# A selective scan and a routed feed-forward block on one core: a shorter routing of tokens, and one product of every second chunk moved from GpSimd to VectorE

## The chip, the core and the metric

The kernel runs on one core of a Trainium2 chip. A core has a matrix engine (TensorE, PE in the profile), a vector engine (VectorE, DVE), a scalar engine (ScalarE, ACT), a general engine (GpSimd, POOL) and a queue that issues transfers (SyncE, SP). The engines run side by side, each through its own instructions in order, and wait for one another by semaphores. The metric is the device time of one execution in microseconds, lower is better. All data are float32; some matmul operands are rounded to fp32r, a form that the matrix engine takes in fewer passes.

## The reference, cut to what matters

The input is 4 sequences of 2048 tokens of width 256. A first block normalises each token, runs a state space scan over time (512 channels, 16 states each) and adds its result to the input. A second block does this, with a router and four small low-rank experts:

```python
logits = einsum('bsd,ed->bse', x, Wg) + bg
scores = softmax(logits)
topv, topi = top_k(scores, 2)
w = sum(one_hot(topi, 4) * topv[..., None], axis=-2)
base = einsum('bsd,fd->bsf', x, Wi)
lora_low = einsum('bsd,erd->bser', x, A)          # 4 experts x rank 4
lora = einsum('bser,efr->bsef', lora_low, B)
h = relu(base[:, :, None, :] + lora)
expert_out = einsum('bsef,df->bsed', h, Wo)
out = einsum('bse,bsed->bsd', w, expert_out)
```

For each token the two experts with the largest logits count. The kernel ranks the four logits, keeps the low-rank row of the best and of the second, and computes only these two. The scan itself is, for each channel and state, `h = h * exp(dt * A) + (dt * x) * B`, and `y = sum over states of h * C`.

## The kernel before

The tokens are cut into 16 chunks of 512 (`NC`), the four sequences in turn. A chunk goes through 16 steps (`STEPS`); a step covers 128 channels (four groups of 32, `J`) and 4 of the 16 states, so that 128 partitions hold 32 channels by 4 states, and four tiles of 128 x 512 lie side by side. In each step:

- GpSimd computes the input of the scan for all four tiles (`times_b`, line 1470, 128 x 2048: `dx_rep` by `b_rep`).
- ScalarE computes the four decays `exp(dt * A)` into the PSUM tiles `decay` (line 1203).
- VectorE scans the four tiles, one instruction each (line 1395). The line reads `decay` from PSUM and `hs` from SBUF.
- The states are multiplied by C. The lower two tiles are always VectorE's (line 1382, 128 x 1024). The upper two are GpSimd's where the step's number modulo 4 is below 3 (`POOL_STEPS`, line 1482), and VectorE's in steps 3, 7, 11 and 15.
- ScalarE copies the last column of each half into `state` (`keep_state`, line 1217). Only then may it write the next step's decays over that half. It waits for the product by C of that half where the scan left the states in `decay`, and for the scan alone where GpSimd takes the product.
- TensorE sums the states (line 998).

On every engine, what else a chunk needs (projections, layer norms, gate, router, feed-forward) is cut into jobs of one letter and one number, and hand-made tables say after which tile of which step each job stands: `PE_SIDE`, `ACT_SIDE`, `DVE_SIDE` and so on for the chunks in general, `..._LAST` for the last chunk, `..._END` for the tail after it. The four cells of a row are the places behind tiles 0 to 3 of that step. `pre`, `post` and `late` mean that the job works for the next chunk, the one before, or the one before that. No planner moves anything: an engine that waits in one job delays all that stands behind it.

The jobs that the change touches:

- H (VectorE, `route`, lines 1325 to 1361; it stands in steps 10 to 12): ten parts. It adds the bias to the logits twice, once into SBUF and once into PSUM, compares all pairs (greater, equal, the lower triangle `tri` for ties), sums to ranks, makes masks, multiplies them into the low-rank rows, and writes the result four times for each choice into `pk`: two copies rounded to fp32r (line 1359), two with what the rounding left (line 1361). Every VectorE instruction of it with two tensors as inputs has one of them in PSUM.
- I (TensorE 951, ScalarE 1170, step 13): four transposes of `pk` and one copy into `low_t`.
- J and S: the experts' matmuls, which read `low_t`.
- X (ScalarE 1166) and M, W: the exponentials and weights of the two choices.
- C0, C1 (step 8, not changed, but of a like form): ScalarE rounds the projection into `dt_st` (line 1093); TensorE subtracts that from the same PSUM bank (line 878); ScalarE copies what is left (line 1086).

Of the kernel before, what the change touches and what calls it, by code (L numbers as in the profile page):

```python
# [41 lines left out]
BOUND = 41.0  # L42

# [156 lines left out]
    "S1 main |  |  | ",  # L200
    " |  |  | H0 post, Y1 main",
    "S2 main, H1 post | H2 post, K2 late, H3 post | H4 post | H5 post",
    "H6 post | H7 post, H8 post | H9 post | M0 post",
# [1355 lines left out]
```

## Time and profile before

| what | us |
|---|---|
| median of 3 runs | 1856.04 |
| the runs | 1853.64, 1856.04, 1858.43 |
| the profiled execution: its own time | 1855.82 |
| its span, first to last instruction | 1854.0 |
| TensorE busy | 1624.7 (88%) |
| VectorE busy | 1763.7 (95%) |
| ScalarE busy | 1503.9 (81%) |
| GpSimd busy | 1714.5 (92%) |

A chunk takes about 108.4 us. Busy time counts an instruction from its start to its end, and neighbours overlap by up to a tenth of a microsecond or more, so what an instruction costs its engine is read from its start to the start of the one behind it. The shares are averages that hold the start (in which GpSimd waits 40.0 us for its first tile) and the tail (from about 1776 us, in which TensorE works and the others wait).

### The profile page before, as it was taken

The numbers are of one execution on the slowest core, as the hardware profiler recorded it, in microseconds if no ns is written. First come the engines' busy times: TensorE is split into PE (matmuls) and PEld (weight loads), VectorE is DVE, ScalarE is ACT, GpSimd is POOL, SyncE is SP. The second block draws the span as 40 slices with busy tenths as digits, with TensorE's granted clock in tenths as the row PEclk, the third lists the DMA queues.
The fourth block names the chain that finished last, engine by engine and source line by source line (L and its number), as shares of the span: only waits on it lengthen the run. The fifth ranks groups of instructions, "written<-read, shape, count | busy, mean of one in ns | idle before, by whom it ended". The sixth has DMA issues, their size and how long they took to land.

```text
span 1854.0 us, 26281 instructions
## 1 busy us (share of the span) xinstructions
PE 1624.7 (88%) x7052; PEld 830.2 (45%) x7052; DVE 1763.7 (95%) x2060; ACT 1503.9 (81%) x3113; POOL 1714.5 (92%) x649
## 2 busy tenths in 40 slices
PE   6657689998998999889898989989899998988999
PEld 3213244444444444444444444444444444444465
DVE  5999999999999999999999999999999999999951
ACT  4776889888898988889898888979888897988643
POOL 1999999999999999999999999999999999999910
PEclk9767799999999999999999999999999999999999
DMA  6655565655656565554747556574665657475200
GB/s 211 138 137 139 118 154 140 157 129 138 152 107 174 131 166 128 141 141 108 181 116 170 140 129 146 111 185 118 165 143 127 137 118 190 99 167 136 63 7 18
DMA packets 150070, 249.07 MB, mean 134 GB/s; under 512 B 22432, under 2 KB 47264, under 8 KB 149408
## 3 DMA queue, kind: packets, MB, share of 16 engines
q1 hardware_dynamic: 145456, 231.09, 51.0%
q0 software_dynamic: 4464, 16.25, 4.6%
q8 instruction: 61, 1.00, 0.2%
q14 instruction: 89, 0.73, 0.1%
HBM read 188.01 MB, written 42.99 MB: 125 GB/s over the span
## 4 chain that ended last, share of the span: by engine, by line
DVE 35%; PE 18%; issue 17%; POOL 16%; ACT 7%; DMA 2%; SPq 1%; DVEq 0%; POOLq 0%; ACTq 0%
DVE decay L1395 15%; POOL hs L1470 10%; DVE hs L1382 9%; DVE hs L1395 7%; POOL hs L1482 4%; PE bank L914 3%; PE bank L962 3%; ACT decay L1203 3%; PE y_ps L998 2%; PE bank L984 2%; POOL z_dt L1450 2%; PE bank L918 1%; DMA b_rep<-bc_scratch 1%; DVE silu L1282 1%; PE bank L979 1%
## 5 line engine op out<-in xcount | busy, mean ns | idle before, releaser
L1470 POOL TENSOR_TENSOR hs<-dx_rep,b_rep 128x2048 f32<-128x2048 f32 x255 | 1188.9, 4678 | 43.1 <-DVE hs L1411 40.0
L1395 DVE TENSOR_TENSOR_SCAN decay<-decay,state,hs 128x512 f32<-128x512 f32 x640 | 791.5, 1270 | 4.9 <-ACT decay L1203 3.9
L1203 ACT ACTIVATE decay<-dt_rep,a_sb 128x512 f32<-128x512 f32 x1024 | 692.5, 685 | 20.6 <-DVE dx_rep L1409 1.8
L1395 DVE TENSOR_TENSOR_SCAN hs<-decay,state,hs 128x512 f32<-128x512 f32 x384 | 485.8, 1265 | 1.3 <-ACT decay L1203 0.8
L1482 POOL TENSOR_TENSOR hs<-hs,c_rep 128x1024 f32<-128x1024 f32 x192 | 476.5, 2482 | 6.0 <-ACT state L1217 5.8
L1382 DVE TENSOR_TENSOR hs<-decay,c_rep 128x1024 f32<-128x1024 f32 x320 | 383.7, 1199 | 0.0
L998 PE MATMUL y_ps<-hs,nsum 128*32 128x512 f32 x2048 | 292.2, 645 | 53.5 <-POOL hs L1482 44.8
L914 PE MATMUL bank<-xn_t,w_in_sb 128*128 128x512 f32 x512 | 252.6, 622 | 10.3 <-DVE silu L1282 3.5
L962 PE MATMUL bank<-w_i_sb,x_t 128*128 128x512 f32 x492 | 249.6, 631 | 8.2 <-DVE silu L1282 6.9
L984 PE MATMUL bank<-w_o_sb,r_t 128*128 128x256 f32 x944 | 217.0, 383 | 4.7 <-ACT r_t L1186 2.7
L984 PEld LDWEIGHTS bank<-w_o_sb,r_t 128*128 128x128 f32 x944 | 178.8, 191 | 56.2 <-issue 28.5
L1217 ACT COPY state<-decay 128x2 f32<-128x2 f32 x320 | 50.6, 158 | 171.0 <-DVE hs L1382 166.3
L914 PEld LDWEIGHTS bank<-xn_t,w_in_sb 128*128 128x128 f32 x512 | 91.9, 195 | 132.4 <-issue 90.4
L962 PEld LDWEIGHTS bank<-w_i_sb,x_t 128*128 128x128 f32 x492 | 89.9, 199 | 121.6 <-issue 89.4
L979 PE MATMUL bank<-ident,r 128*128 128x128 f32 x920 | 120.8, 278 | 6.4 <-ACT r L1181 4.3
L979 PEld LDWEIGHTS bank<-ident,r 128*128 128x128 f32 x920 | 100.6, 141 | 52.2 <-DVE x L1298 15.6
L936 PE MATMUL bank<-w_out_sb,gated 128*128 128x256 f32 x496 | 118.0, 380 | 0.3 <-DVE gated L1287 0.3
L998 PEld LDWEIGHTS y_ps<-hs,nsum 128*32 128x32 f32 x2048 | 41.9, 110 | 148.2 <-issue 125.6
L1181 ACT ACTIVATE r<-bank,wgt 128x512 f32<-128x512 f32 x123 | 83.1, 675 | 23.5 <-PE bank L885 23.4
L936 PEld LDWEIGHTS bank<-w_out_sb,gated 128*128 128x128 f32 x496 | 94.5, 191 | 14.0 <-DVE gated L1287 0.7
L1177 ACT ACTIVATE r<-bank,wgt 128x512 f32<-128x512 f32 x123 | 83.1, 676 | 20.0 <-PE bank L966 19.6
L1186 ACT COPY r_t<-bank 128x512 f32<-128x512 f32 x119 | 69.4, 583 | 17.8 <-PE bank L979 13.4
(170 smaller groups left out, 1823.9 us busy)
## 6 DMA issues: line engine op xcount, KB each, us to landing
dx_rep<-rep_scratch SPq DMA_DIRECT2D x252, 256.0 KB, 4.7
dt_rep<-rep_scratch SPq DMA_DIRECT2D x252, 256.0 KB, 7.6
b_rep<-bc_scratch SPq DMA_DIRECT2D x256, 64.0 KB, 4.0
c_rep<-bc_scratch SPq DMA_DIRECT2D x256, 64.0 KB, 2.4
rep_scratch<-z_dt SPq DMA_DIRECT2D x64, 256.0 KB, 2.6
rep_scratch<-e_dt SPq DMA_DIRECT2D x64, 256.0 KB, 2.7
e_dt<-z_dt POOLq DMA_DIRECT2D x31, 512.0 KB, 4.6
xin<-in_u SPq DMA_DIRECT2D x16, 512.0 KB, 4.1
```

What stands on the lines that cost most here:

```text
L914: mm = pe.matmul(ps[:], w_in_sb[:, k, col:col + P], xn_t[odd][:, k, :], start=k == 0, stop=k == KD - 1)
L936: pe.matmul(ps[:, cols], gated[odd][:, k, i * P:(i + 1) * P], w_out_sb[:, k, :], start=k == 0 and is_last(q) and i % 2 == 0, stop=False, s ...
L962: pe.matmul(ps[:], x2_t[odd][:, k, t * P:(t + 1) * P], w_i_sb[:, k, cols], start=k == 0, stop=False, skip_group_check=is_last(q))
L979: mm = pe.matmul(ps[:, f * P:(f + 1) * P], r[i % 2][:, f * P:(f + 1) * P], ident[:], start=r is r1, stop=r is r2, is_transpose=True)
L984: mm = pe.matmul(ps[:, 0:D], r_t[:, f, :], w_o_sb[:, f, :], start=f == 0, stop=f == NF - 1)
L998: mm = pe.matmul(y_ps[32 * j:32 * j + 32, :], nsum[:], hs[s % 4][:, j, :], start=k == 0, stop=k == KG - 1, skip_group_check=True)
L1177: nc.scalar.activation(r1[i % 2][:], ps[:], ACT.Relu, scale=wgt[odd][:, 0, i // 2:i // 2 + 1]).then_inc(r1_ready, 1)
L1203: nc.scalar.activation(decay[:, j, :], dt_rep[m % 2][:, j, :], ACT.Exp, scale=a_sb[:, J * s + j:J * s + j + 1]).then_inc(decay_ready, 1)
L1382: v.tensor_tensor(hs[s % 4][:, js, :], decay[:, js, :], c_rep[:, k, :].unsqueeze(1).to_broadcast([P, 2, T]), ALU.mult).then_inc(prod_vecto ...
L1395: v.tensor_tensor_scan(hs[s % 4][:, j, :] if kept else decay[:, j, :], decay[:, j, :], hs[s % 4][:, j, :], state[:, b, n:n + 1], ALU.mult, ...
L1470: nc.gpsimd.tensor_tensor(hs[s % 4][:], dx_rep[m % 2][:], b_rep[:, k, :].unsqueeze(1).to_broadcast([P, J, T]), ALU.mult).then_inc(input_re ...
L1482: nc.gpsimd.tensor_tensor(hs[s % 4][:, 2:4, :], hs[s % 4][:, 2:4, :], c_rep[:, k, :].unsqueeze(1).to_broadcast([P, 2, T]), ALU.mult).then_ ...
```

## The change

1. The routing has seven parts (H0 to H6). The biased logits are written once, in SBUF. A difference of all pairs replaces the two comparisons; ties are settled by comparing with a tiny number instead of zero. Both masks come from one instruction. One instruction applies them to the low-rank rows. The instructions from the pair differences to the masks now have both inputs in SBUF.
2. ScalarE writes `pk` (new job H0 on ScalarE, a copy of `low` repeated four times, 128 x 512) and frees the bank.
3. `pk` is no longer rounded by VectorE. The transposes leave the raw values in the bank; ScalarE copies them rounded into `low_t` (I0), TensorE subtracts the rounded values from half of the rows by a matmul with `neg_low` (new job I1), and ScalarE copies the bank once more (new job I1).
4. `POOL_STEPS` loses step 14. In even chunks the upper product by C of step 14 stays on GpSimd, in odd ones it is VectorE's, with a semaphore of its own.
5. The tables: H7 to H9 go; ScalarE's H0 stands behind tile 2 of step 12, its I1 behind I0 in the same cell of step 13; TensorE's I1 stands behind E3 in step 13. K3 and S3 change places on VectorE in step 14, T0 stands one cell earlier on ScalarE in step 0. The tables of the last chunk and of the tail are shifted in a like way.
6. VectorE makes `neg_low` once at the start, with two small instructions, and fills two columns of `ranks`.

```diff
-    "K2 late, H7 post | H8 post | H9 post | M0 post",
+    "K2 late |  |  | M0 post",
...
-    " | J7 late, S7 late | T6 late, X0 post | T7 late",
-    " | I0 post | E3 main | V3 main",
+    " | J7 late, S7 late | T6 late, X0 post, H0 post | T7 late",
+    " | I0 post, I1 post | E3 main | V3 main",
...
-    " | I0 post, E3 main, K3 late, J0 post, D2 pre",
+    " | I0 post, E3 main, I1 post, K3 late, J0 post, D2 pre",
...
+TURN_STEP = 14
+POOL_STEPS = [s for s in range(STEPS) if s % KG < 3 and s != TURN_STEP]
...
+                if letter == "I" and i == 1:
+
+                    pe.wait_ge(low_hi, q + 1)
+                    pe.matmul(banks[used("I0", c, AHEAD[when])[0]][:], neg_low[:], low_t[:], start=False, stop=True,
+                              skip_group_check=True).then_inc(low_rest, 1)
...
+                elif letter == "H":
+                    act.wait_ge(low_ready, q + 1)
+                    nc.scalar.copy(pk[:].rearrange("p t a b w -> p (t a) b w"),
+                                   low[:].rearrange("p t a w -> p (t a) w").unsqueeze(2).to_broadcast([P, 2 * TT, 4, NE * LR])
+                                   ).then_inc(freed[used("H0", c, AHEAD[when])[0]], 1)
+                elif letter == "I" and i == 1:
+                    act.wait_ge(low_rest, q + 1)
+                    b, _ = used("I0", c, AHEAD[when])
+                    nc.scalar.activation(low_t[:], banks[b][:], ACT.Identity).then_inc(freed[b], 1)
                 elif letter == "I":
                     at_least(act, z2_ready, NP * q)
-                    ps, free = wait_filled(act, job[:2], c, when)
-                    nc.scalar.activation(low_t[:], ps[:], ACT.Identity).then_inc(free, 1)
+                    ps, _ = wait_filled(act, job[:2], c, when)
+                    nc.scalar.activation(low_t[:], ps[:], ACT.Identity).then_inc(low_hi, 1)
...
+                    last = v.tensor_tensor(lg[:], z[:, :, 0:NE], b_g_sb[:], ALU.add)
...
+                    last = v.tensor_tensor(gap[:], lg[:].unsqueeze(2).to_broadcast(grid), lg[:].unsqueeze(3).to_broadcast(grid),
+                                           ALU.subtract)
...
+                    v.tensor_tensor(lm[:, :, 0:NE], lg[:], mx[:].unsqueeze(2).to_broadcast([P, TT, NE]), ALU.subtract)
+                    last = v.scalar_tensor_tensor(out=gt[:], in0=tri[:], scalar=-TINY, in1=gap[:], op0=ALU.mult, op1=ALU.is_lt)
...
+                    last = v.tensor_reduce(rank[:], gt[:].rearrange("p t e f -> p (t e) f"), AX, ALU.add)
...
+                    last = v.tensor_tensor(sel[:, 0::2], rank[:].unsqueeze(1).to_broadcast([P, 2, TT * NE]),
+                                           ranks[:].unsqueeze(2).to_broadcast([P, 2, TT * NE]), ALU.is_equal)
...
+                    v.tensor_tensor(own2[:], lm[:, :, 0:NE], sel[:, 2].rearrange("p (t e) -> p t e", t=TT), ALU.mult)
+                    last = v.tensor_tensor(sel[:, 1], sel[:, 2], sel[:, 0], ALU.subtract)
...
+                    v.tensor_reduce(lm[:, :, NE], own2[:], AX, ALU.add).then_inc(router, 1)
+                    shape = [P, 2, TT, NE, LR]
+                    last = v.tensor_tensor(
...
-            def times_c(c, s, h):
-
-                if (s, h) not in V_PAIRS:
+            def times_c(c, s, h, odd):
+
+                if h == 1 and on_pool(s, odd):
                     return
```

**ScalarE, steps 12 and 13 of a chunk.** `decay` is the exponential of a tile, `state` the copy of last columns. Before:

```order
L1217 COPY state<-decay 128x2
L1203 ACTIVATE decay<-dt_rep,a_sb 128x512
L1166 ACTIVATE pexp<-lm 128x20
L1203 ACTIVATE decay<-dt_rep,a_sb 128x512
L1217 COPY state<-decay 128x2
L1203 ACTIVATE decay<-dt_rep,a_sb 128x512 x2
L1170 ACTIVATE low_t<-bank 128x512
L1217 COPY state<-hs 128x2
L1203 ACTIVATE decay<-dt_rep,a_sb 128x512
```

And of the change:

```order
L1253 COPY state<-decay 128x2
L1236 ACTIVATE decay<-dt_rep,a_sb 128x512
L1190 ACTIVATE pexp<-lm 128x20
L1193 COPY pk<-low 128x512
L1236 ACTIVATE decay<-dt_rep,a_sb 128x512
L1253 COPY state<-decay 128x2
L1236 ACTIVATE decay<-dt_rep,a_sb 128x512 x2
L1203 ACTIVATE low_t<-bank 128x512
L1199 ACTIVATE low_t<-bank 128x512
L1253 COPY state<-hs 128x2
L1236 ACTIVATE decay<-dt_rep,a_sb 128x512
```

A copy into `pk` stands ahead of the fourth decay of step 12, and a second copy into `low_t`, which waits for TensorE, ahead of the third decay of step 13.

**VectorE, steps 12 and 13.** `SCALAR_TENSOR_TENSOR` with `state` is a scan. Before:

```order
L1382 TENSOR_TENSOR hs<-decay,c_rep 128x1024
L1351 TENSOR_REDUCE bank<-own 128x4
L1352 TENSOR_TENSOR bank<-bank,change 128x4x16
L1395 SCALAR_TENSOR_TENSOR decay<-decay,state,hs 128x512
L1358 TENSOR_TENSOR lm<-bank,mx 128x4
L1359 CAST pk<-bank 128x16x16
L1395 SCALAR_TENSOR_TENSOR hs<-decay,state,hs 128x512
L1382 TENSOR_TENSOR hs<-decay,c_rep 128x1024
L1361 TENSOR_TENSOR pk<-bank,pk 128x16x16
L1395 SCALAR_TENSOR_TENSOR hs<-decay,state,hs 128x512
L1369 TENSOR_REDUCE sm<-pexp 128x4
L1395 SCALAR_TENSOR_TENSOR decay<-decay,state,hs 128x512 x2
```

And of the change:

```order
L1401 TENSOR_TENSOR hs<-decay,c_rep 128x1024
L1414 SCALAR_TENSOR_TENSOR decay<-decay,state,hs 128x512
L1414 SCALAR_TENSOR_TENSOR hs<-decay,state,hs 128x512
L1401 TENSOR_TENSOR hs<-decay,c_rep 128x1024
L1414 SCALAR_TENSOR_TENSOR hs<-decay,state,hs 128x512
L1388 TENSOR_REDUCE sm<-pexp 128x4
L1414 SCALAR_TENSOR_TENSOR decay<-decay,state,hs 128x512 x2
```

Five small instructions between the scans of step 12 are gone.

**VectorE, steps 14 and 15 of an odd chunk.** Before:

```order
L1395 SCALAR_TENSOR_TENSOR hs<-decay,state,hs 128x512
L1382 TENSOR_TENSOR hs<-decay,c_rep 128x1024
L1395 SCALAR_TENSOR_TENSOR hs<-decay,state,hs 128x512
L1395 SCALAR_TENSOR_TENSOR decay<-decay,state,hs 128x512 x3
L1382 TENSOR_TENSOR hs<-decay,c_rep 128x1024
```

And of the change:

```order
L1414 SCALAR_TENSOR_TENSOR decay<-decay,state,hs 128x512 x2
L1401 TENSOR_TENSOR hs<-decay,c_rep 128x1024
L1414 SCALAR_TENSOR_TENSOR decay<-decay,state,hs 128x512 x2
L1401 TENSOR_TENSOR hs<-decay,c_rep 128x1024
L1414 SCALAR_TENSOR_TENSOR decay<-decay,state,hs 128x512 x2
L1401 TENSOR_TENSOR hs<-decay,c_rep 128x1024
```

The upper product of step 14 stands behind the first scan of step 15, as those of steps 3, 7, 11 and 15 do.

## Rows read from the trace of the kernel before

**Rows 1.** Page, part 1: busy time of each engine.

```profile
PE 1624.7 (88%) x7052; PEld 830.2 (45%) x7052; DVE 1763.7 (95%) x2060; ACT 1503.9 (81%) x3113; POOL 1714.5 (92%) x649
```

**Rows 2.** Busy time by stretch: from:to, length, then each engine's busy time.

```profile
1150.00:1259.00 109.00, 98.27 (x439) 50.71 (x437) 108.98 (x127) 94.14 (x197) 108.30 (x42) 1.00 0.61 144
```

**Rows 3.** Waits, whole run: who waited for whom, total, times, longest.

```profile
DVE decay L1395 <- ACT decay L1203: 3.9, 4, 1.8
DVE decay L1395 <- POOL hs L1470: 0.7, 2, 0.5
```

**Rows 4.** Timeline of GpSimd, steps 9 and 10: start, duration, instruction.

```profile
1177.87 4.55 POOL L1470 TENSOR_TENSOR hs<-dx_rep,b_rep 128x2048 f32<-128x2048 f32 x1
1182.60 4.54 POOL L1470 TENSOR_TENSOR hs<-dx_rep,b_rep 128x2048 f32<-128x2048 f32 x1 [0.18 <-PE y_ps L998]
1187.08 2.39 POOL L1482 TENSOR_TENSOR hs<-hs,c_rep 128x1024 f32<-128x1024 f32 x1
1189.42 4.54 POOL L1470 TENSOR_TENSOR hs<-dx_rep,b_rep 128x2048 f32<-128x2048 f32 x1
```

**Rows 5.** Timeline of VectorE: the first scan of step 9.

```profile
1183.88 1.26 DVE L1395 TENSOR_TENSOR_SCAN decay<-decay,state,hs 128x512 f32<-128x512 f32 x1
```

**Rows 6.** Timeline of VectorE, steps 12 and 13.

```profile
1206.68 0.16 DVE L1351 TENSOR_REDUCE bank<-own 128x4 f32<-128x16 f32 x1
1206.76 0.22 DVE L1352 TENSOR_TENSOR bank<-bank,change 128x64 f32<-128x64 f32 x1
1206.89 1.28 DVE L1395 TENSOR_TENSOR_SCAN decay<-decay,state,hs 128x512 f32<-128x512 f32 x1
1208.08 0.15 DVE L1358 TENSOR_TENSOR lm<-bank,mx 128x4 f32<-128x4 f32 x1
1208.13 0.41 DVE L1359 CAST pk<-bank 128x256 fp32r<-128x256 f32 x1
1208.46 1.27 DVE L1395 TENSOR_TENSOR_SCAN hs<-decay,state,hs 128x512 f32<-128x512 f32 x1
1209.65 1.19 DVE L1382 TENSOR_TENSOR hs<-decay,c_rep 128x1024 f32<-128x1024 f32 x1
1210.77 0.41 DVE L1361 TENSOR_TENSOR pk<-bank,pk 128x256 f32<-128x256 f32 x1
1211.10 1.27 DVE L1395 TENSOR_TENSOR_SCAN hs<-decay,state,hs 128x512 f32<-128x512 f32 x1
1212.35 2.46 DVE L1395 TENSOR_TENSOR_SCAN decay<-decay,state,hs 128x512 f32<-128x512 f32 x2
1214.71 1.26 DVE L1395 TENSOR_TENSOR_SCAN hs<-decay,state,hs 128x512 f32<-128x512 f32 x1
```

**Rows 7.** Timeline of ScalarE, steps 12 and 13.

```profile
1208.55 0.68 ACT L1203 ACTIVATE decay<-dt_rep,a_sb 128x512 f32<-128x512 f32 x1
1210.88 0.16 ACT L1217 COPY state<-decay 128x2 f32<-128x2 f32 x1 [1.14 <-DVE hs L1382]
1211.07 1.30 ACT L1203 ACTIVATE decay<-dt_rep,a_sb 128x512 f32<-128x512 f32 x2
1212.31 0.57 ACT L1170 ACTIVATE low_t<-bank 128x512 fp32r<-128x512 f32 x1
1213.00 0.69 ACT L1203 ACTIVATE decay<-dt_rep,a_sb 128x512 f32<-128x512 f32 x1
```

**Rows 8.** Timeline of ScalarE, step 8: C0 and C1.

```profile
1176.21 0.68 ACT L1093 ACTIVATE dt_st<-bank,b_x_sb 128x512 fp32r<-128x512 f32 x1
1177.84 0.68 ACT L1086 ACTIVATE dt_st<-bank,b_x_sb 64x512 fp32r<-64x512 f32 x1 [0.36 <-PE bank L878]
```

**Rows 9.** Instructions on the tile dt_st: TensorE's subtraction, shortest, median, longest in ns.

```profile
L878 PE MATMUL bank<-dt_st,neg_id x16: 468/796/796, 24.8 to 1610.8; 128*128 128x512 f32 x16
```

**Rows 10.** Timeline of ScalarE: the copy behind the last job of step 15.

```profile
1230.44 0.16 ACT L1217 COPY state<-decay 128x2 f32<-128x2 f32 x1 [0.56 <-DVE hs L1382]
```

**Rows 11.** Groups of instructions of VectorE: the product by B at the start.

```profile
L1411 DVE TENSOR_TENSOR hs<-dx_rep,b_rep 128x1024 f32<-128x1024 f32 x2 | 2.5, 1225 | 0.1
```

More of the change, by code:

```diff
@@ L198 @@
     " |  | K1 late, Y0 main | ",
+    " |  | S1 main | ",
     " |  |  | ",
[L200 to L203, printed above, removed]
+    " | Y1 main |  | H0 post",
+    "S2 main, H1 post, H2 post | K2 late, H3 post | H4 post | H5 post",
+    "H6 post |  |  | M0 post",
     "K3 late, M1 post |  |  | ",
@@ L349 @@
 BANKS = 3
-POOL_STEPS = [s for s in range(STEPS) if s % KG < 3]
-V_PAIRS = [(s, h) for s in range(STEPS) for h in range(2) if h == 0 or s not in POOL_STEPS]
+TURN_STEP = 14
+POOL_STEPS = [s for s in range(STEPS) if s % KG < 3 and s != TURN_STEP]
+V_PAIRS = [(s, h) for s in range(STEPS) for h in range(2) if h == 0 or s not in POOL_STEPS + [TURN_STEP]]
 BANK_JOBS = "ABCDEFGHIJTK"
-LAST_H = 9
+LAST_H = 6
 LOOP_FROM, LOOP_TO = 3, 3 + 2 * BATCH
@@ L415, in bank_jobs @@
                     name = {"Y": "F", "Z": "J"}.get(name[0], name[0]) + name[1]
-                if name[0] in BANK_JOBS and name != "C1":
+                if name[0] in BANK_JOBS and name not in ("C1", "I1"):
                     yield name, when, J * s + j
@@ L426, in freed_at @@
         engine, by = "dve", name
-    elif letter == "C":
-        engine, by = "act", "C1"
+    elif letter in "CI":
+        engine, by = "act", letter + "1"
     elif letter == "E":
@@ L431, in freed_at @@
     elif letter == "H":
-        engine, by = "dve", f"H{LAST_H}"
+        engine, by = "act", "H0"
     else:
@@ L522, in block_program @@
         neg_id = sb("neg_id", [P, P], F32R)
+        neg_low = sb("neg_low", [P, P], F32R)
         b_g_sb = sb("b_g_sb", [P, TT, NE])
@@ L616, in block_program, with on_pool @@
         NEWTON_STEPS = 4
+        def on_pool(s, odd):
+            return s in POOL_STEPS or s == TURN_STEP and not odd
         def vector_products(c, s, h):
@@ L950, in job_pe @@
                     for t in range(TT):
-                        mm = pe.transpose(ps[:, t * P:(t + 1) * P], pk[:, t].rearrange("p a b c d -> p (a b c d)"), ident[:])
+                        mm = pe.matmul(ps[:, t * P:(t + 1) * P], pk[:, t].rearrange("p a b w -> p (a b w)"), ident[:],
+                                       start=t == 0, stop=False, is_transpose=True, skip_group_check=True)
                 elif letter in "ZJ":
@@ L1210, in keep_state @@
                 js = slice(2 * h, 2 * h + 2)
-                if h == 1 and s in POOL_STEPS:
+                if h == 1 and on_pool(s, b % 2):
                     act.wait_ge(scan_done, UNITS * c + J * (s + 1))
                     last = hs[s % 4][:, js, T - 1]
+                elif h == 1 and s == TURN_STEP:
+                    act.wait_ge(turn_product, c + 1)
+                    last = decay[:, js, T - 1]
                 else:
@@ L1227, in _ @@
                 v.memset(consts[:, n], value)
+            for rank_of in range(2):
+                v.memset(ranks[:, rank_of:rank_of + 1], float(rank_of))
             v.memset(bound[:], BOUND).then_inc(zeroed, 1)
@@ L1365, in weigh_choices @@
+                last.then_inc(low_ready if i == LAST_H else mask_step, 1)
             def weigh_choices(i, q, odd):
@@ L1382, in times_c @@
                 v.tensor_tensor(hs[s % 4][:, js, :], decay[:, js, :], c_rep[:, k, :].unsqueeze(1).to_broadcast([P, 2, T]),
-                                ALU.mult).then_inc(prod_vector, 1)
+                                ALU.mult).then_inc(turn_product if h == 1 and s == TURN_STEP else prod_vector, 1)
             def scan(c, b, s, j):
@@ L1418, in body @@
                         v.tensor_scalar(neg_id[:], ident[:], -1.0, None, ALU.mult)
+                        for part in range(2):
+                            v.tensor_scalar(neg_low[:].rearrange("p (x c w) -> p x c w", x=4, c=2)[:, :, part],
+                                            ident[:].rearrange("p (x c w) -> p x c w", x=4, c=2)[:, :, part], -float(part), None,
+                                            ALU.mult)
                         split_weights(w_dt_st, hs[1][:, 0, :], 1)
@@ L1471, in times_b, with times_c @@
                                         ALU.mult).then_inc(input_ready, 1)
-            def times_c(c, s):
-                if s not in POOL_STEPS:
+            def times_c(c, s, odd):
+                if not on_pool(s, odd):
                     return
```

91 lines of the change are left out of this document (35 added, 56 removed), and 41 rows, old and new, of tables (ACT_END, ACT_LAST, ACT_SIDE, DVE_SIDE).

## The prediction, made before the change was run

> **What bounds the kernel now.** I read the page first. VectorE is busy 95% of the span and GpSimd 92% [rows 1]; the busy table by stretch then shows that in the middle of the run both are full: of 109.00 us VectorE works 108.98, GpSimd 108.30, ScalarE 94.14 [rows 2]. A chunk takes 108.4 us. To see which of the two sets the pace I went to the list of waits. VectorE waits for ScalarE's decays 3.9 us in the whole run and for GpSimd's inputs 0.7 us [rows 3]. So VectorE works without a pause, each of its instructions lies on the path, and a microsecond taken from or given to it moves the end by one. GpSimd is nearly as full, but never late.
>
> How much room lies between the two, the timelines tell. GpSimd's product by B for step 9 starts at 1177.87 and costs 4.49 (from 1182.60 to 1187.08 for the next of its kind), so it is done at 1182.36 [rows 4]; VectorE's first scan of step 9 starts at 1183.88 [rows 5]. GpSimd is 1.5 us ahead at what is the tightest step of a chunk.
>
> ScalarE is a third party that the shares hide. Its decays of a step cannot start before VectorE has multiplied the half that lies in their place. In the timelines the product of step 12 gives VectorE free at 1210.77 [rows 6], ScalarE copies the state at 1210.88 and starts two decays at 1211.07, I0 at 1212.31, the third decay of step 13 at 1213.00, which is done at 1213.69 [rows 7]; VectorE scans that tile at 1214.71 [rows 6]. It has 1.02 us to spare there.
>
> **The routing on VectorE.** What an instruction costs is the distance to the next start: 256 elements 0.33, 64 elements 0.13, a reduction from 16 to 4 elements 0.07 to 0.08, 4 elements 0.05, a scan 1.18 to 1.19, a product by C 1.12 [rows 6]. A 16-element one I put at 0.08 (between 0.05 and 0.13). Before, the routing is 19 instructions: 2 of 256 elements (0.66), 7 of 64 (0.91), 10 small ones (0.77): 2.34 us. After, it is 11: one of 128 elements (between 0.13 and 0.33, taken as 0.20), 3 of 64 (0.39), one of 32 (0.09), 6 small ones (0.48): 1.16 us. Saved: 1.18 us a chunk. The routing of 15 chunks lies beside scans, that of the last one in the tail: 15 x 1.18 = 17.7 us less.
>
> **The upper product of step 14.** In 8 odd chunks VectorE gets one more product, 8 x 1.12 = 9.0 us more. GpSimd loses 2.34 us each time [rows 4], which is worth nothing by itself, since it isn't late. In the other chunks nothing changes; the separate semaphore costs no instruction.
>
> Behind it, ScalarE's third decay of step 15 must now wait for this product, as in step 3. Counted from the product's end, ScalarE needs 0.11 + 0.19 for the copy of the state, two decays at 0.62, J1, S0 and the two halves of D3 at 0.57 each: 3.82 us, then 0.19 and 0.69 until the first decay of the next step is there, 4.70 in all. VectorE has two scans, a product and a scan to do, 4.69. Today ScalarE idles 0.56 us at this place [rows 10]; that room goes, and VectorE waits 0.05 us or so, 0.5 us over 8 chunks. The bound above is a S0 that waits for TensorE as C1 does, 0.36 [rows 8]: 3 us.
>
> **The copy into pk (ScalarE, step 12).** ScalarE idles 1.14 us ahead of 1210.88 [rows 7]. VectorE comes there sooner by what is gone in between, H7 (0.21) and H8 (0.05 + 0.33), and the copy costs 0.48 to 0.57 by the like instruction, I0 (duration 0.57 [rows 7]). 1.14 - 0.59 - 0.57 leaves nothing, but not less than nothing: I count it as hidden, with up to 0.15 us a chunk if not.
>
> **The second pass of I (step 13).** Here I expect the loss. ScalarE's I1 stands in the cell of I0, and it waits for TensorE's subtraction, which waits for I0. The trace has this form in C0 and C1: C0 ends at 1176.21 + 0.68 = 1176.89 and C1 starts at 1177.84 [rows 8], a round trip of 0.95 us, 0.80 of it the matmul at its median, 0.47 at its shortest [rows 9]. C0 and C1 have a decay between them that fills two thirds of that; I0 and I1 have nothing, and all that stands behind them on ScalarE waits: a copy of the state and the third decay. TensorE will have E3 behind it by then, since pk is written by about 1209.1 (the copy takes the place of the decay of 1208.55) and not at 1211.18 (1210.77 + 0.41). Count it: I0 starts at 1212.31 and ends at 1212.88, I1 starts 0.95 later at 1213.83, and if it costs what I0 does up to the decay (0.69), that decay starts at 1214.52 and is done at 1215.21. VectorE wants it at 1214.71 - 0.33 = 1214.38, since the 0.33 us of H9 between the product and the scans are gone [rows 6]. It waits 0.83 us. With the shortest matmul the trip is 0.62 and the wait 0.50; with the copy into pk late as well it is 1.0. I take 0.83, since the median and longest matmul agree. 15 x 0.83 = 12.5 us.
>
> **Start and tail.** The start gets two small instructions for neg_low (0.3 us). In the tail TensorE is full; the shorter routing frees VectorE, which waits anyway, and I1 adds one matmul, 0.5 us. I take 1.0 us for the two, with -1 and +2 as bounds.
>
> **The sum.** -17.7 + 9.0 + 0.5 + 12.5 + 1.0 = +5.3, of which I take off 0.5 because the last chunk's I0 and I1 stand a step earlier, where less hangs on them: +4.8 us. The profiled execution took 1855.82 us, 1854.0 of it the span, 0.2 less than the median of the runs, 1856.04. Put on the median this gives 1860.8 us.
>
> **A rule against this change.** No row shows a VectorE instruction with two SBUF inputs beside a working GpSimd. The product by B at the start is one [rows 11], and GpSimd has no work yet; in the middle of the run each of VectorE's instructions with two tensors takes one from PSUM, and their cost doesn't move at all while GpSimd works without a pause. The new routing has six with both inputs in SBUF (the pair differences, lm, gt, the masks, own2, the difference of the masks). The Trainium skill (SBUF — State Buffer, "Who interferes with whom") says that VectorE's second SBUF input comes through a read interface shared with GpSimd, and that whichever of the two starts second is blocked until the other's instruction is through. By that rule the price is the third rival below.
>
> **Rivals.**
>
> *The trip is hidden.* If ScalarE's round trip costs VectorE nothing, the 12.5 us fall away: -7.7, 1848.3 us. For it: ScalarE is idle 15 of 109 us [rows 2]. Against it: that time lies elsewhere, and the order at this place is fixed.
>
> *Odd and even chunks don't average out.* An even chunk is short on VectorE (108.4 - 1.2 = 107.2) and still 108.2 on GpSimd, an odd one the other way round (108.3 and 105.9). If each is set by its longer engine nothing is won: 1856 us. The 1.5 us of lead [rows 4, 5] speak against it, since the even chunk uses up 1.0.
>
> *VectorE waits for GpSimd's reads (the case that ends slower).* The place is the routing in steps 10 to 12. GpSimd reads SBUF all the time, in instructions of 4.49 and 2.34 us [rows 4]; one that is met at a random time has on average (16 x 4.49² + 14 x 2.34²) / (2 x 108.4) = 1.84 us to go. Four places with one or two such instructions each wait 4 x 1.84 = 7.4 us, six single waits 11.0 us a chunk, all on VectorE and on the path. Over 15 chunks that is 111 to 165 us, on top of 1848.3 (the wait at step 13 then lies in theirs): 1959 to 2013 us, about 1985. It decides from 0.15 us a wait on, even with the trip hidden (15 x 6 x 0.15 = 13.5 us). For it: nothing else in the kernel does this, so the flat costs say nothing about it. Against it: only that no row shows such a block.
>
> **How the numbers follow.** My forecast 0.50, the hidden trip 0.22, no averaging 0.08, the blocked reads 0.20. A measurement of this kernel tells 0.3% (5.6 us, so 1850.5 and 1861.6) from no change. My forecast, from 1855 to 1868 with its bounds (0.50 to 1.0 at step 13, up to 3 at step 15), lies two thirds within and one third above. Within: 0.33 + 0.07 = 0.40; slower: 0.17 + 0.20 = 0.37; faster 0.23 with the hidden trip and a little of the rest. The range from 1846 to 1875 holds the first three cases and leaves out the blocked reads, 2 in 10.
>
> **What would show it.** In the changed profile: VectorE's routing at 1.1 to 1.2 us a chunk; on ScalarE, about 0.95 us between I0's end and I1's start, in every chunk; on VectorE, a gap of 0.8 us ahead of the third scan of step 13, put down to ScalarE's decay, and the total of that wait up from 3.9 to some 16 us; GpSimd idle 1 to 2 us a chunk and waiting for VectorE; periods of about 108.1 us in even and 109.2 in odd chunks. I am wrong if that gap is missing, if the small VectorE instructions last microseconds instead of 0.1 to 0.3, or if VectorE waits for GpSimd's inputs.

## The result and the profile after

The changed kernel takes 2024.8 us in the median, the kernel before 1855.1 (measured again beside it): a ratio of 1.094, 95% interval 1.091 to 1.097, 170 us slower. The forecast was 1860.8 us with a range of 1846 to 1875. What came was the third rival: VectorE's instructions with two inputs in SBUF wait for GpSimd.

The page of the changed kernel, busy times, against [rows 1] and [rows 2]:

```profile
PE 1667.2 (83%) x7068; PEld 846.3 (42%) x7068; DVE 1910.1 (95%) x1944; ACT 1518.3 (75%) x3145; POOL 1699.7 (84%) x641
```

and its stretch from 1150 to 1259 us (busy time of PE, PEld, DVE, ACT, POOL, then granted clock, DMA share, GB/s):

```profile
1150.00:1259.00 109.00, 95.49 (x419) 49.56 (x418) 108.40 (x114) 89.29 (x185) 99.61 (x39) 0.95 0.55 126
```

VectorE has 116 instructions fewer and is busy 146 us longer; GpSimd, busy 92% of the span before, is busy 84% and now waits. So VectorE's instructions themselves have grown. The groups of its routing name them (total, mean in ns, idle time before):

```profile
L1361 DVE TENSOR_TENSOR gap<-lg 128x64 f32<-128x64 f32 x16 | 59.8, 3740 | 0.0
L1365 DVE TENSOR_TENSOR lm<-lg,mx 128x16 f32<-128x16 f32 x16 | 30.1, 1883 | 0.1
L1374 DVE TENSOR_TENSOR sel<-sel 128x16 f32<-128x16 f32 x16 | 26.3, 1645 | 0.0
L1373 DVE TENSOR_TENSOR own<-lm,sel 128x16 f32<-128x16 f32 x16 | 26.1, 1629 | 0.0
L1370 DVE TENSOR_TENSOR sel<-rank,ranks 128x32 f32<-128x32 f32 x16 | 19.9, 1245 | 0.0
L1366 DVE SCALAR_TENSOR_TENSOR gt<-tri,gap 128x64 f32<-128x64 f32 x16 | 5.6, 351 | 0.0
L1378 DVE TENSOR_TENSOR low<-bank,sel 128x128 f32<-128x128 f32 x16 | 4.4, 277 | 0.0
```

The six with both inputs in SBUF take 167.8 us; the seventh, twice as large but with one input in PSUM, takes 0.28 us each time. The block, as the wait of such a read for GpSimd is called here, doesn't show as idle time: it stands in the duration of the blocked instruction. The timelines of one chunk show what ends it. VectorE (start, duration):

```profile
1182.89 4.56 DVE L1361 TENSOR_TENSOR gap<-lg 128x64 f32<-128x64 f32 x1
1187.38 0.74 DVE L1320 SCALAR_TENSOR_TENSOR silu<-bank,b_in_sb,e_gate 128x512 f32<-128x512 f32 x1
1188.04 1.67 DVE L1365 TENSOR_TENSOR lm<-lg,mx 128x16 f32<-128x16 f32 x1
1189.63 0.21 DVE L1366 SCALAR_TENSOR_TENSOR gt<-tri,gap 128x64 f32<-128x64 f32 x1
...
1194.66 0.16 DVE L1373 TENSOR_TENSOR own<-lm,sel 128x16 f32<-128x16 f32 x1
1194.73 0.17 DVE L1374 TENSOR_TENSOR sel<-sel 128x16 f32<-128x16 f32 x1
```

GpSimd in the same stretch, which answers to [rows 4]:

```profile
1182.87 4.50 POOL L1493 TENSOR_TENSOR hs<-dx_rep,b_rep 128x2048 f32<-128x2048 f32 x1
1187.33 2.33 POOL L1505 TENSOR_TENSOR hs<-hs,c_rep 128x1024 f32<-128x1024 f32 x1
1194.74 0.88 POOL L1483 DMA_DIRECT2D e_dt<-z_dt  x1 [5.08 <-ACT e_dt L1137]
1195.36 4.83 POOL L1493 TENSOR_TENSOR hs<-dx_rep,b_rep 128x2048 f32<-128x2048 f32 x1
```

GpSimd's product starts at 1182.87, the pair differences 0.02 us later, and they end together, at 1187.4. The next read, lm, ends with the next product at 1189.7. From there GpSimd is idle for 5.08 us, and the same kind of instruction passes in 0.16. In 12 of 15 chunks the pair differences meet the product by B at its very start and last 4.54 to 4.57 us. In six chunks one of the last three reads falls behind GpSimd's DMA start. GpSimd in another chunk:

```profile
1423.76 0.89 POOL L1483 DMA_DIRECT2D e_dt<-z_dt  x1 [4.83 <-ACT e_dt L1137]
1424.37 4.84 POOL L1493 TENSOR_TENSOR hs<-dx_rep,b_rep 128x2048 f32<-128x2048 f32 x1
1428.85 2.65 POOL L1473 TENSOR_TENSOR z_dt<-e_dt,x_t 128x1024 f32<-128x1024 f32 x1
1431.14 4.79 POOL L1493 TENSOR_TENSOR hs<-dx_rep,b_rep 128x2048 f32<-128x2048 f32 x1
```

and VectorE:

```profile
1423.90 0.16 DVE L1373 TENSOR_TENSOR own<-lm,sel 128x16 f32<-128x16 f32 x1
1423.98 12.00 DVE L1374 TENSOR_TENSOR sel<-sel 128x16 f32<-128x16 f32 x1
```

A subtraction of 16 elements waits through three GpSimd instructions and is let in at 1435.9, when GpSimd has nothing left to do. It stands there already before the first of the three is recorded to start. Five chunks hold such a wait of 11.9 to 12.0 us, and in all five the read starts 0.20 to 0.32 us behind the DMA's start and 0.29 to 0.41 us ahead of the product behind it (own2, above, starts 0.14 us behind the DMA's start and still passes); their periods are 126 to 129 us, most others 114 to 116, against 108.4 before. The Trainium skill (SBUF — State Buffer, "Who interferes with whom") has the block, up to the end of the other's instruction; the 12.00 us row goes beyond what it says.

What was forecast for step 13 stands in this trace too: I0 (1204.09 + 0.58), I1 0.58 us later, and VectorE's wait for the decay behind them.

```profile
1204.09 0.58 ACT L1203 ACTIVATE low_t<-bank 128x512 fp32r<-128x512 f32 x1
1205.25 0.60 ACT L1199 ACTIVATE low_t<-bank 128x512 fp32r<-128x512 f32 x1 [0.58 <-PE bank L898]
```

```profile
1206.69 1.28 DVE L1414 TENSOR_TENSOR_SCAN hs<-decay,state,hs 128x512 f32<-128x512 f32 x1 [0.59 <-ACT decay L1236]
```

### The profile page after: what moved, and what is told of

Its sections match the earlier page's. It is cut to its first block, busy times and chain, and to the rows that moved or that the text cites. A ratio compares the mean times of both kernels' runs of the same rounds, so it can differ in the third digit from the quotient of the medians.

```text
span 2020.1 us, 26173 instructions
## 1 busy us (share of the span) xinstructions
PE 1667.2 (83%) x7068; PEld 846.3 (42%) x7068; DVE 1910.1 (95%) x1944; ACT 1518.3 (75%) x3145; POOL 1699.7 (84%) x641
## 4 chain that ended last, share of the span: by engine, by line
DVE 49%; PE 20%; issue 18%; ACT 7%; POOL 2%; DVEq 0%; ACTq 0%; POOLq 0%
DVE decay L1414 19%; DVE hs L1401 10%; DVE hs L1414 9%; PE bank L1005 4%; PE bank L983 3%; PE y_ps L1022 3%; ACT decay L1236 3%; DVE gap L1361 3%; PE bank L934 2%; PE bank L1000 2%; DVE silu L1320 2%; POOL hs L1493 1%; DVE gated L1325 1%; DVE sel L1374 1%; DVE own L1373 1%
## 5 line engine op out<-in xcount | busy, mean ns | idle before, releaser
L1414 DVE TENSOR_TENSOR_SCAN decay<-decay,state,hs 128x512 f32<-128x512 f32 x656 | 814.9, 1278 | 7.9 <-ACT decay L1236 6.2
L1505 POOL TENSOR_TENSOR hs<-hs,c_rep 128x1024 f32<-128x1024 f32 x184 | 447.5, 2432 | 81.7 <-ACT state L1253 76.6
L1414 DVE TENSOR_TENSOR_SCAN hs<-decay,state,hs 128x512 f32<-128x512 f32 x368 | 468.6, 1273 | 16.8 <-ACT decay L1236 16.6
L1401 DVE TENSOR_TENSOR hs<-decay,c_rep 128x1024 f32<-128x1024 f32 x328 | 395.7, 1206 | 0.0
L1022 PE MATMUL y_ps<-hs,nsum 128*32 128x512 f32 x2048 | 301.0, 663 | 69.1 <-POOL hs L1505 40.3
L983 PE MATMUL bank<-w_i_sb,x_t 128*128 128x512 f32 x484 | 265.3, 675 | 59.9 <-DVE silu L1320 58.3
L1005 PE MATMUL bank<-w_o_sb,r_t 128*128 128x256 f32 x976 | 222.8, 382 | 4.6 <-ACT r_t L1219 2.6
L1000 PE MATMUL bank<-ident,r 128*128 128x128 f32 x912 | 126.9, 290 | 55.0 <-DVE x L1336 50.3
L1000 PEld LDWEIGHTS bank<-ident,r 128*128 128x128 f32 x912 | 106.8, 148 | 101.5 <-DVE x L1336 65.8
```

Source lines behind the costliest of these rows:

```text
L983: pe.matmul(ps[:], x2_t[odd][:, k, t * P:(t + 1) * P], w_i_sb[:, k, cols], start=k == 0, stop=False, skip_group_check=is_last(q))
L1000: mm = pe.matmul(ps[:, f * P:(f + 1) * P], r[i % 2][:, f * P:(f + 1) * P], ident[:], start=r is r1, stop=r is r2, is_transpose=True)
L1005: mm = pe.matmul(ps[:, 0:D], r_t[:, f, :], w_o_sb[:, f, :], start=f == 0, stop=f == NF - 1)
L1022: mm = pe.matmul(y_ps[32 * j:32 * j + 32, :], nsum[:], hs[s % 4][:, j, :], start=k == 0, stop=k == KG - 1, skip_group_check=True)
L1401: v.tensor_tensor(hs[s % 4][:, js, :], decay[:, js, :], c_rep[:, k, :].unsqueeze(1).to_broadcast([P, 2, T]), ALU.mult).then_inc(turn_produ ...
L1414: v.tensor_tensor_scan(hs[s % 4][:, j, :] if kept else decay[:, j, :], decay[:, j, :], hs[s % 4][:, j, :], state[:, b, n:n + 1], ALU.mult, ...
```

## The experiments

### The blocked reads: taken away, and put in alone

Theory: VectorE's second SBUF input is what GpSimd blocks. Rivals: the alternation, the new order, or the new instructions themselves.

**The changed kernel with one input of each in PSUM.** The edit, in short form (lgp, gapp and rankp lie in the router's PSUM bank):

```
-  gap[:] = lg - lg           + gapp = lgp - lg
-  lm = lg - mx               + lm = lgp - mx
-  gt = tri * -TINY < gap     + gt = tri * -TINY < gapp
-  sel[0], sel[2] = rank == 0, 1     + sel[0] = rankp == 0
-  own2 = lm * sel[2]         + own2 = (rankp == 1) * lm
-  sel[1] = sel[2] - sel[0]   + sel[1] = (rankp == 1) - sel[0]
```

> The changed kernel, with one input of each of the six routing instructions that read two SBUF tensors now in PSUM (logits, pair differences and ranks in the router's bank); one small instruction more, the order of all jobs as in the changed kernel. If VectorE's second SBUF input is what GpSimd blocks: the waits of 1 to 5 us in the routing go, it costs 1.2 to 1.4 us a chunk again, and the kernel takes about 1861 us (1848 to 1870), my forecast for the change. If instead the new order, the round trip of I0 and I1 or the alternation of step 14 makes the loss, or the new instructions are slow in themselves: 1990 us or more.

Measured 1865.2 us, ratio 1.0041 (1.0026 to 1.0056). Its rows in place of those of 3740 and 1883 ns:

```profile
L1366 DVE TENSOR_TENSOR bank<-bank,lg 128x64 f32<-128x64 f32 x16 | 3.5, 219 | 0.0
L1370 DVE TENSOR_TENSOR lm<-bank,mx 128x16 f32<-128x16 f32 x16 | 2.6, 161 | 0.1
```

Same order, same alternation, one instruction more, and 160 us are gone. The loss was the second SBUF input. (Kernels in this form, with one input of each read in PSUM, are called clean below, and this one the first clean kernel.) All GpSimd instructions that a read was held behind read SBUF themselves; no run has one that doesn't, so whether GpSimd's reading or its mere working blocks is not shown here.

**Without the alternation** (TURN_STEP = -1), and **the alternation alone** on the kernel before:

> The changed kernel without the alternation: step 14's upper product is always GpSimd's. If the blocked reads make the loss: VectorE is rid of 8 x 1.12 = 9 us, but GpSimd is busier, so that a read meets it more often; between 2010 and 2025 us. If the alternation makes the loss: about 1855 us.

> The kernel before with the alternation of step 14 alone. By the sum of the prediction: 8 x 1.12 + 0.5 = +9.5 us, 1864 to 1866 us. If the alternation is the loss: 1990 us or more. If even and odd chunks don't average out in the way of the sum because GpSimd sets part of the pace: +4 to +9 us.

1998.0 us (1.0755, 1.0728 to 1.0783) and 1866.7 us (1.0055, 1.0043 to 1.0067). Alone, the alternation costs 10.7 us, near the forecast 9.5. In the changed kernel it costs 27, and the expectation of 2010 to 2025 us failed. The six executions without it lie between 1981 and 2026 us, so the 27 is rough. The changed kernel's trace holds six waits beyond 5 us behind the DMA start (five of 12), the one without alternation three, but that trace is of the fastest execution. That the alternation costs more here because it shifts where the reads meet GpSimd is likely and not shown.

**One single read.** In the kernel before, the greater-than table is kept in SBUF:

```
-  gtp = ps[:, 96:160]...
+  gtp = gt[:]
```

> The kernel before with one change: the greater-than table of the routing is kept in SBUF instead of PSUM, so that one of VectorE's instructions in a chunk (the addition of 64 elements) reads two SBUF tensors. Theory: it waits for the end of the GpSimd instruction under way, 0 to 4.5 us, 1.84 at a random time: +28 us over 15 chunks, 1883 us; anything from 1857 to 1920, since it meets GpSimd at about the same phase each time. Rival: one such read does no harm, or its cost lies in the new kernel's instructions: 1854 to 1857.

1885.4 us (1.0159, 1.0141 to 1.0176), 29.8 us for one added read in a chunk; the estimate was 28. VectorE and GpSimd:

```profile
1105.82 2.20 DVE L1339 TENSOR_TENSOR gt<-gt,eq 128x64 f32<-128x64 f32 x1
```

```profile
1103.39 4.54 POOL L1470 TENSOR_TENSOR hs<-dx_rep,b_rep 128x2048 f32<-128x2048 f32 x1
1107.90 2.34 POOL L1482 TENSOR_TENSOR hs<-hs,c_rep 128x1024 f32<-128x1024 f32 x1
```

It starts 2.1 us ahead of the product's end and ends with it. It isn't random: 13 of the 15 chunks show 2.16 to 2.20 us, so that the estimate from a random meeting came so near is luck. The edit also moves the table's writing to SBUF (line 1331, one input in PSUM); that instruction keeps its 0.21 us, so it is the read that waits and not the write.

### How long a read is held

**GpSimd's product by B in halves**, in the changed kernel:

```
-  g.tensor_tensor(hs[all 4 tiles])
+  g.tensor_tensor(hs[tiles 0, 1]); g.tensor_tensor(hs[tiles 2, 3])
```

> The changed kernel with each of GpSimd's products by B as two instructions of half the size. Theory (VectorE is blocked to the end of the GpSimd instruction that is reading): the wait at the pair differences falls from 4.5 us to at most 2.3, some 2.2 x 15 = 33 us less, about 1990 us, as far as the long blocks stay alike. Rival (blocked until GpSimd pauses or signals): the wait stays at 4.5 us, 2020 us or more.

2078 us (1.120, 1.116 to 1.124). The wait at the pair differences did fall, from 3740 to 2200 ns in the mean, in most chunks to 1.0 to 1.5 us, up to the end of the one instruction under way. So the rival's wait of 4.5 us did not come, though the total lies where the rival had put it. The theory's own total failed by 88 us: the rows behind moved against GpSimd, and the comparison of the ranks now falls behind the DMA start, mostly 7.6 us long.

```profile
L1370 DVE TENSOR_TENSOR sel<-rank,ranks 128x32 f32<-128x32 f32 x16 | 86.0, 5373 | 0.0
L1361 DVE TENSOR_TENSOR gap<-lg 128x64 f32<-128x64 f32 x16 | 35.2, 2200 | 0.0
```

**The changed kernel without GpSimd's DMA V0:**

```
+  if i == 0: return        # in job V, ahead of the accumulating DMA
```

> The changed kernel without GpSimd's accumulating DMA V0 in step 11 (it leaves out that addition for the first half of the channels from the second chunk on). Theory: a VectorE read that is caught while GpSimd starts a DMA and the three products behind it isn't let in between them; without the DMA the blocks of 9.6 to 12 us go and none is longer than one GpSimd instruction, 4.6 us; about 1950 us. Rival: the long blocks come from several GpSimd instructions that stand ready one behind the other, with or without a DMA: some stay, 1990 us or more.

2043.3 us (1.100, 1.098 to 1.103). The long blocks went, as the theory has it: of 48 waits none is longer than 4.6 us. The time, 1950 us by the theory, didn't follow: without the DMA's 0.6 us GpSimd starts its next product earlier, 0.56 us ahead of own2 in one chunk (352.91 and 353.47), so that own2 waits for most of it in nearly every chunk, 3520 ns in the mean, where it mostly passed before.

**One read behind the DMA.** Since the two runs had moved too much at once, a single read in the kernel before, the same once more without V0:

```
-  second = ps[:, 240:244]
+  second = sm[:]           # read in lm[:, :, NE] = second - mx, step 12
```

> The kernel before with one change: the second-largest logits (4 elements) are kept in SBUF, so that the subtraction in step 12, 5 us behind GpSimd's DMA start, reads two SBUF tensors. Theory (held from the DMA until GpSimd pauses): VectorE waits until GpSimd has used up what it can do without VectorE, one or two products by B and the dx product, 5 to 9 us a chunk: +75 to +135 us, about 1960. Rival (to the end of the one instruction under way): 0 to 4.5 us, at a random time 1.84: +28, at most 1923 us.

> The same with GpSimd's DMA V0 left out (that addition is not made for the first half of the channels from the second chunk on). Theory: without the DMA the read is let in at the end of one GpSimd instruction, at most 4.6 us: between 1855 and 1923 us, and 28 us above the kernel before if it meets GpSimd at random. Rival (the DMA has no part in it): as long as with it.

With the DMA 1953.6 us (1.052, 1.051 to 1.054), without it 1896.4 (1.021, 1.019 to 1.023). VectorE and GpSimd with it:

```profile
1152.19 7.16 DVE L1358 TENSOR_TENSOR lm<-sm,mx 128x4 f32<-128x4 f32 x1
```

```profile
1147.15 0.84 POOL L1460 DMA_DIRECT2D e_dt<-z_dt  x1
1147.76 4.80 POOL L1470 TENSOR_TENSOR hs<-dx_rep,b_rep 128x2048 f32<-128x2048 f32 x1
1152.26 2.62 POOL L1450 TENSOR_TENSOR z_dt<-e_dt,x_t 128x1024 f32<-128x1024 f32 x1
1154.57 4.75 POOL L1470 TENSOR_TENSOR hs<-dx_rep,b_rep 128x2048 f32<-128x2048 f32 x1
1164.28 2.35 POOL L1482 TENSOR_TENSOR hs<-hs,c_rep 128x1024 f32<-128x1024 f32 x1 [4.96 <-ACT state L1217]
```

The read is not let in at the ends at 1152.6 and 1154.9 and is let in at 1159.3, when GpSimd itself has to wait (for ScalarE's copy of the state, which comes behind VectorE's scan). 13 of the first 14 chunks with this read are like it (7.1 to 8.6 us); in the other one GpSimd pauses at the first end. Without the DMA, VectorE and GpSimd:

```profile
1239.36 1.89 DVE L1358 TENSOR_TENSOR lm<-sm,mx 128x4 f32<-128x4 f32 x1
```

```profile
1238.83 2.39 POOL L1450 TENSOR_TENSOR z_dt<-e_dt,x_t 128x1024 f32<-128x1024 f32 x1
1241.16 4.53 POOL L1472 TENSOR_TENSOR hs<-dx_rep,b_rep 128x2048 f32<-128x2048 f32 x1
```

Nine of 14 are let in at the first end, five run on to GpSimd's pause, 6.4 us: the expected bound of 4.6 us was wrong for these. So with the DMA start the read was held past the first end whenever GpSimd had more to do, but the DMA start isn't the only cause. What the rows of both sides differ in is how far GpSimd's next instruction is recorded as started before the last one ends. Counted over seven traces, without ends that fall within 0.05 us of the read's own start: where that overlap is 0.25 to 0.36 us, as it is behind a DMA start (1152.26 + 2.62 - 1154.57 = 0.31), VectorE was let in at none of 77 ends; where it is 0.03 to 0.11, at 134 of 146. All 77 lie within 13 us behind a DMA start, so these rows don't tell the overlap and the DMA start apart. What decides among the 146 stays open.

### The rest of the forecast, priced in the clean kernel

Three kernels with one input in PSUM: step 14 all on GpSimd; the same with I1 moved on ScalarE,

```
-  " | I0 post, I1 post | E3 main | V3 main",
+  " | I0 post | I1 post, E3 main | V3 main",
```

and that move with the alternation kept:

> The first of these kernels (one input of each in PSUM) and no alternation. By the sum: 9.5 us less than with the alternation, about 1851 us, with GpSimd as the next bound at 108.2 us a chunk; between 1848 and 1856. If GpSimd is the bound without the alternation it takes 1855 us or more. If the step 13 trip costs nothing, 1843.

> As the kernel with one input in PSUM and step 14 on GpSimd (1858.2 us), with ScalarE's second pass I1 moved behind the third decay of step 13. If the round trip costs what the trace shows, 0.44 to 0.63 us ahead of the third scan in 15 chunks, it is 7 to 9 us faster as long as GpSimd (107.4 us a chunk) allows it: 1850 to 1853. If GpSimd sets the pace already (it is busy 108.5 of 109 us), the stall turns into another wait and nothing is won: 1857 to 1859.

> The kernel with one input in PSUM and the alternation (1865.2 us), with I1 moved behind the third decay of step 13. The stall that goes is 0.44 us in each of 15 chunks. If it was on the path there (GpSimd isn't full in every second chunk): 6.6 us less, about 1858.5 us. If TensorE's or GpSimd's limits take it back: 1863 to 1866.

1858.2 us (1.0008, 0.9998 to 1.0017), 1857.5 (1.0008, 0.9998 to 1.0018) and 1856.1 (0.9992, 0.9981 to 1.0003). The move is worth 9 us with the alternation and nothing measurable without. Without it GpSimd sets the pace: in the second of these kernels its products by B come round in 108.1 to 108.3 us in 12 of 14 chunks (the 107.4 in that kernel's expectation is too low). And the last chunk takes part of the gain back: from its first scan to the end it is 188.0 to 189.2 us in the traces of the kernel before, the alternation alone and the two clean kernels with I1 in place, and 190.4 to 192.9 in all six with I1 moved. VectorE's wait ahead of the first scan of step 13 there, in the first clean kernel, is 1.75 us, with I1 moved 2.83 to 2.85; in the kernel before it doesn't wait for ScalarE there:

```profile
1763.68 2.47 DVE L1420 TENSOR_TENSOR_SCAN decay<-decay,state,hs 128x512 f32<-128x512 f32 x2 [1.75 <-ACT decay L1236]
```

A chunk in the middle of the second kernel, without any stall of VectorE over 0.3 us (columns as above):

```profile
902.20:1010.50 108.30, 98.35 (x436) 50.83 (x436) 107.71 (x120) 94.63 (x198) 107.83 (x42) 0.98 0.60 148
```

What was left over in the middle chunks were waits of 1.2 to 3.2 us ahead of the second scan of step 0 in some chunks (the expectations below call the place step 15). VectorE, ScalarE and TensorE there in the first clean kernel, behind an odd chunk:

```profile
1350.62 1.29 DVE L1420 TENSOR_TENSOR_SCAN decay<-decay,state,hs 128x512 f32<-128x512 f32 x1 [1.23 <-ACT decay L1236]
```

```profile
1349.40 0.60 ACT L1219 COPY r_t<-bank 128x512 f32<-128x512 f32 x1 [1.92 <-PE bank L1000]
```

```profile
1343.75 0.53 PE L905 MATMUL bank<-lora_st,low_t 64*128 64x512 f32 x1 [1.92 <-ACT r L1210]
1344.33 3.54 PE L983 MATMUL bank<-w_i_sb,x_t 128*128 128x512 f32 x4
...
1351.11 1.98 PE L983 MATMUL bank<-w_i_sb,x_t 128*128 128x512 f32 x4
```

and the busy table of the place, with the granted clock:

```profile
1342.00:1344.00 2.00, 0.25 (x1) 0.18 (x1) 2.00 (x3) 1.76 (x4) 2.00 (x2) 1.00 1.09 312
1344.00:1346.00 2.00, 1.96 (x3) 0.83 (x3) 2.00 (x3) 2.00 (x5) 2.00 (x2) 0.52 0.92 209
1346.00:1348.00 2.00, 2.00 (x4) 0.52 (x2) 1.88 (x2) 1.39 (x4) 2.00 (x1) 0.63 0.10 32
1348.00:1350.00 2.00, 2.00 (x17) 1.73 (x16) 1.38 (x2) 0.60 (x2) 0.50 (x1) 1.00 0.00 0
```

TensorE stood still for 1.92 us, then its granted clock fell to half (0.52 in the mean of the slice from 1344), the level of 1.2 GHz; four matmuls took 3.54 us in place of 1.98, its transposes came late, ScalarE's copy waited for them, and behind the copy the decay. The next kernels shorten the pause by making the first matmul of J1 twice:

```
+  if letter == "J" and i == 1 and not is_last(q):
+      pe.matmul(ps, x2_t[..., 0, ...], w_i_sb[:, 0, cols], start=True, stop=False)
```

> As before, but VectorE takes step 14's upper product in one chunk of four instead of in two. By the sum of instructions GpSimd needs 108.2 us a chunk without alternation and VectorE 107.3; with a quarter it is 108.2 - 2.34/4 = 107.6 and 107.3 + 1.12/4 = 107.6. If GpSimd is what held the kernel without alternation (1857.5 us): 0.6 x 15 = 9 us less, about 1848 us. If the delays behind TensorE's fallen clock (1.2 to 3.2 us each) set the time: 1853 to 1858.

> The kernel with a quarter of alternation, and one matmul of J1 made twice (0.99 us of TensorE work that changes no result), so that TensorE's pause of 1.8 us in front of step 15 shortens to 0.8. If the pauses bring the falls of its clock to half, there are fewer behind step 15 and VectorE's waits of 1.2 to 3.2 us there go: up to 5 us less than without, 1843 to 1848. If the clock falls for another cause, or the extra work is late itself: the same or up to 5 us more.

> The kernel without alternation and with I1 behind the decay (1857.5 us), and the same extra matmul. If GpSimd's 108.2 us a chunk hold it, the falls of the clock hide behind that and removing them wins nothing: 1855 to 1858 us. If the falls add up with it: 1848 to 1853.

> The kernel with one input in PSUM, the alternation in every second chunk and I1 behind the decay (1856.1 us), with one matmul of J1 made twice. Its periods are 107.3 and 108.5 us but for three waits of 1.9 to 2.0 us where TensorE's clock had fallen. If the extra matmul takes these away as it did with a quarter of alternation: 4 to 6 us less, 1850 to 1852 us. If they only move: 1854 to 1857.

In the first of these, "as before" means the clean kernel with the alternation and I1 moved. A quarter of alternation alone won nothing (1858.0 us; 0.9998, 0.9988 to 1.0008): 9 us were expected. With the matmul it takes 1854.2 (0.9980, 0.9971 to 0.9989), 3.8 less; the waits of 1.4 to 2.0 us ahead of that scan became 0.7 or went. That is the one kernel faster than the kernel before, by 0.2%; its expectation was 1843 to 1848. Where GpSimd holds the pace the matmul wins nothing (1858.9 us; 1.0005, 0.9996 to 1.0015), as its expectation has it; in the alternating kernel neither (1856.7; 1.0002, 0.9993 to 1.0011), against 1850 to 1852: the two waits of 1.9 and 2.0 us at this scan went, but two of 1.6 and 0.7 us stand there in other chunks, and the third wait, ahead of the first scan of step 0, stayed (2.4 us; the kernel before has it too, 1.8). So what the extra matmul is worth is open: it gained in one kernel of three.

## Why the prediction was wrong

**The step that failed** is the price of the six reads: the term "The routing on VectorE" counts them at 0.08 to 0.13 us each, as if one input still lay in PSUM (1.16 us a chunk for the whole routing), and they took 167.8 us over the run, 10 us a chunk more than that. What let it fail is the weighing in "A rule against this change" and "How the numbers follow": the block got a chance of 0.20 and was left out of the range, because no row of before showed one. But no row could: in the kernel before nothing reads two SBUF tensors beside a working GpSimd, which the prediction had itself noted. Absence from a trace that can't contain the thing is no evidence against it; the rule spoke of exactly this form, and the six new instructions have it.

**The rival's own sum held** better than its chance. It asked 7.4 to 11.0 us a chunk; the six instructions took 167.8 us, in PSUM form their six successors take 16.9 (2.5 to 3.5 each), and the difference of 150.9 is 10.1 us in each of the 15 chunks (in the 16th, in the tail, none lasts over 0.22 us). It lay 12 us short of the measured time at its upper end because its base was 1848.3 where the clean kernel takes 1865.2, and because the waits for decays at steps 12 and 13 grew. VectorE's waits in the changed kernel:

```profile
DVE hs L1414 <- ACT decay L1236: 16.6, 27, 1.5
```

and in the clean one (total, times, longest):

```profile
DVE hs L1420 <- ACT decay L1236: 7.0, 15, 0.8
```

The rival's mean wait, a random meeting, was wrong in kind: four of six reads wait nothing in most chunks, one waits 1.5 us (it lasts 1.67), one 4.3 (4.55), and in five chunks one waits 12. That the sum came out right is in good part luck. It also said that the rival decides from 0.15 us a wait on; the smallest common wait was ten times that.

**VectorE as the bound, each microsecond on the path:** right for additions (one read of 2.0 us more: 29.8 us over 15 chunks), wrong for savings. The room ahead of GpSimd was read from one step [rows 4, 5] as 1.5 us; it is used up once, and then GpSimd's 108.2 us a chunk hold, 0.2 below the 108.4 of the kernel before. The prediction had worked out that number in its second rival and given it 0.08; with what the last chunk loses it took the gain of the kernels without alternation.

**The routing:** 2.34 to 1.16 us was forecast; start to start it is 2.28 before and 1.16 in the first clean kernel: right there, and far off in the changed kernel, as said above.

**Step 14:** +9.0 and 0.5; alone it measured 10.7 (8.0 to 12.4 by the interval). Right. In the first clean kernel no wait over 0.3 us is seen at step 15, as forecast. But behind five of the eight odd chunks VectorE waits 1.2 to 1.45 us at step 0, 6.6 in all, each time behind a pause of TensorE of 1.7 to 2.1 us and a fall of its clock, which the prediction left out.

**The copy into pk:** hidden, as forecast; no wait of VectorE stands at step 12 in the clean kernel.

**The second pass of I:** right in place and kind, a wait ahead of the third scan of step 13 in 14 chunks. It was sized 0.83 us by the matmul's median; the trip took 0.59, near the shortest matmul's 0.62, and the wait was 0.44 in the clean kernel, 6.2 over 14 chunks (the row above has 7.0 and 15 times because it holds one wait at the start, 0.85 us, that the kernel before has too). The whole term, forecast 12.5, measured 9 when I1 was moved away, a move that also took away three of the five waits at step 0 told above. In the last chunk the prediction took 0.5 us off because less hangs on I0 and I1 there; the clean kernel's trace has the wait of 1.75 us shown above instead.

**Start and tail:** +1.0 was forecast; from the last chunk's first scan to the end it is 188.7 us before and 188.8 in the clean kernel, so what the last chunk loses by that wait it gets back elsewhere, and the two together give nothing.

Together the forecast of +4.8 us is that of the clean kernel, which measured +9.2 (4.8 to 10.4 by its interval). Its parts as measured are -16.9 (15 x 1.127) for the routing, +10.7 for the alternation, +6.2 for the second pass and +6.6 for the waits at step 0, an estimate of +6.6 us: the second pass was put too high, and the waits behind the clock were put at nothing. The forecast described a kernel in which VectorE's reads are free.

## What to carry to other kernels

Before moving a tensor of VectorE's from PSUM to SBUF, count its SBUF inputs: with two of them and a GpSimd that works beside it, a 16-element instruction that met a GpSimd instruction lasted 1.7 to 12 us in place of 0.16. Look for it in the instruction's own duration; the waits don't show it. When the trace of before can't contain an effect, take its chance from the rule and the form of the new instructions, and let the range reach it. And before counting a saving on the fullest engine, sum up the chunk of the second fullest.
